# Down products m4, m5 and m7: the half-filled last chunk laid on both partition halves, two matmuls for it instead of three

## The reference, cut to what matters

```
mod = silu(c) @ wmod                        # six vectors per batch
x = x + ga * ((layernorm(x)*(1+ca)+sa) @ masked_weight.T)
h = layernorm(x)*(1+cb)+sb
u = silu(h @ w1.T) * (h @ w2.T)             # 2048 x 2752; w1, w2, w3 are 4-bit codes with scales
x = x + gb * (u @ w3.T)                     # the down product: 2752 summed over, 1024 out
```

## Time and profile before

| what | us |
|---|---|
| median of three runs | 1569.66 |
| span of the profiled execution | 1567.6 |
| down stage, first to last matmul | 1144.7 to 1563.7 |
| TensorE busy in the span | 1539.4 |
| VectorE busy in the span | 1029.5 |

### The profile page before, as it was taken

The page is one execution under the profiler, slowest core; times in us unless marked ns, Lnnn a source line. Parts: engine busy times, 40 slices in busy tenths (PEclk is TensorE's granted clock), DMA queues, the critical chain, the costliest instruction groups (busy, mean ns, idle before and its releaser), DMA issues.

```text
span 1567.6 us, 19154 instructions
## 1 busy us (share of the span) xinstructions
PE 1539.4 (98%) x7200; PEld 1269.6 (81%) x7200; DVE 1029.5 (66%) x1486; ACT 989.6 (63%) x1290; POOL 5.5 (0%) x10
## 2 busy tenths in 40 slices
PE   5899999999999999999999999999999999999999
PEld 3688888888888888888888888888888888888887
DVE  5687786555555455547676666666875757956994
ACT  3475676998888888884898988785433432333220
POOL 0000000000000000000000000000000000000000
PEclk9999999999999999999999999999999999999999
DMA  9976423564555445532778787786777868947973
GB/s 368 372 258 228 134 81 138 177 200 166 186 169 187 153 162 180 178 128 97 257 228 252 207 250 208 207 254 171 260 292 272 332 204 302 343 160 268 397 279 122
DMA packets 170139, 345.97 MB, mean 221 GB/s; under 512 B 14752, under 2 KB 65344, under 8 KB 170048
## 3 DMA queue, kind: packets, MB, share of 16 engines
q1 hardware_dynamic: 170048, 344.76, 65.1%
HBM read 249.77 MB, written 94.93 MB: 220 GB/s over the span
## 4 chain that ended last, share of the span: by engine, by line
PE 96%; DMA 2%; DVE 0%; ACT 0%; SPq 0%; issue 0%
PE ps L1916 10%; PE ps L1915 10%; PE ps L1914 10%; PE ps L1988 9%; PE ps L1987 9%; PE ps L1989 9%; PE ps L1925 9%; PE ps L1927 9%; PE ps L1926 9%; PE ps L1832 4%; PE ps L1834 4%; PE ps L1833 4%; DMA wmod<-wmod 2%; PE ps L1789 2%; PE ps L1772 1%; DVE attn_w_lo L1368 0%
## 5 line engine op out<-in xcount | busy, mean ns | idle before, releaser
L861 ACT ACTIVATE w_raw<-w_raw 128x1024 f32<-128x1024 f32 x287 | 304.6, 1061 | 9.1
L1914 PE MATMUL ps<-ffn_in_hi,w_hi 128*128 128x512 f32 x688 | 268.6, 390 | 0.0
L1916 PE MATMUL ps<-ffn_in_hi,w_lo 128*128 128x512 f32 x688 | 267.8, 389 | 0.0
L1915 PE MATMUL ps<-ffn_in_lo,w_hi 128*128 128x512 f32 x688 | 267.7, 389 | 0.0
L1987 PE MATMUL ps<-t_hi,s_hi 128*128 128x512 f32 x616 | 239.6, 389 | 0.0
L1988 PE MATMUL ps<-t_lo,s_hi 128*128 128x512 f32 x616 | 239.6, 389 | 0.0
L1989 PE MATMUL ps<-t_hi,s_lo 128*128 128x512 f32 x616 | 239.6, 389 | 0.0
L1925 PE MATMUL ps<-x_m_hi,stream_hi 128*128 128x512 f32 x604 | 235.0, 389 | 0.0
L1926 PE MATMUL ps<-x_m_lo,stream_hi 128*128 128x512 f32 x604 | 235.0, 389 | 0.0
L1927 PE MATMUL ps<-x_m_hi,stream_lo 128*128 128x512 f32 x604 | 235.0, 389 | 0.0
L1114 ACT ACTIVATE s_hi<-s_raw 128x1408 fp32r<-128x1408 f32 x56 | 77.4, 1383 | 241.2 <-DVE s_raw L1624 192.6
(11 more groups left out here) (136 smaller groups left out, 2078.1 us busy)
## 6 DMA issues: line engine op xcount, KB each, us to landing
s_raw<-h_d SPq DMA_DIRECT2D x96, 704.0 KB, 5.6
stream_raw<-t_d SPq DMA_DIRECT2D x150, 256.0 KB, 3.4
t_d<-combined SPq DMA_DIRECT2D x106, 256.0 KB, 2.6
wmod<-wmod SPq DMA_DIRECT2D x12, 2048.0 KB, 15.3
t_raw<-w_d SPq DMA_DIRECT2D x88, 256.0 KB, 6.1
w_codes<-w12q SPq DMA_DIRECT2D x41, 512.0 KB, 5.3
h_d<-h_tile SPq DMA_DIRECT2D x44, 256.0 KB, 2.4
h_d<-up_c SPq DMA_DIRECT2D x44, 256.0 KB, 3.3
```

The source lines that it names most:

```text
L861: act.activation(RAWF[r], RAWF[r] if j else RQ[r][:], ACT.Prelu, bias=bias, scale=sign, alpha=slope).then_inc(line_ready, 1)
L1914: pe.matmul(acc, RH[r][:, k, :], HH[:, b, k, :], start=(k == 0), stop=False)
L1915: pe.matmul(acc, RH[r][:, k, :], HL[:, b, k, :], start=False, stop=False)
L1916: last = pe.matmul(acc, RL[r][:, k, :], HH[:, b, k, :], start=False, stop=(k == C - 1))
```

## The change

A list `SHORT_K` marks m4, m5 and m7. For these:
- `load_s` takes 10 chunks in one DMA, and the last chunk's 64 filled rows in a second one whose source is read twice, `[2, 64, 128]`, so that they land on partitions 0 to 63 and again on 64 to 127.
- `load_t` reads the last chunk's 64 filled rows twice, `[2, 64, columns]`, in the same way.
- `s_low` writes S_lo of the last chunk over the lower half of S_hi, and S_lo of the other ten as before: two instructions.
- `t_low` sets the lower half of T_lo's last chunk to zero and subtracts the upper 64 rows.
- `down_tile` then needs two matmuls for the last chunk: (S_hi over S_lo) x (T_hi twice) and (S_hi over S_lo) x (T_lo over zero).

```diff
...
     TWO_S = [len(p[1]) == 2 for p in PRODUCTS]
     TWO_T = [len(p[3]) == 2 for p in PRODUCTS]
     COPIES = 4
+    SHORT_K = [p[0] in ("m4", "m5", "m7") for p in PRODUCTS]
 
     def s_adds(m):
         return sum(JT for i in range(m // JT) if TWO_S[i]) + (m % JT + 1 if TWO_S[m // JT] else 0)
 
     def s_loads(m):
-        return 16 * sum(len(PRODUCTS[n // JT][1]) for n in range(m % 4, m + 1, 4))
+        return 16 * sum(len(PRODUCTS[n // JT][1]) * (2 if SHORT_K[n // JT] else 1) for n in range(m % 4, m + 1, 4))
 
     def one_row(i):
         blocks = PRODUCTS[i][3]
...
                 sp.wait_ge(w3_combined, j + 1)
                 sp.dma_start(w3_d[j * P:(j + 1) * P, :], E3[j % 3][:]).then_inc(w3_stored[j % 3], 16)
 
+            def twice(rows):
+                return rows.unsqueeze(0).broadcast_to([2, TAIL, rows.shape[1]])
+
             def load_s(m):
                 p = m % 4
                 if m >= 4:
...
                 blocks = PRODUCTS[m // JT][1]
                 for n, (r, half) in enumerate(blocks):
                     tile = (half - 1) * TILES + (r - 1) * JT + m % JT
-                    sp.dma_start(SR[p][:, 1 - n].rearrange("p c k -> p (c k)"),
-                                 h_d[tile * P:(tile + 1) * P, :]).then_inc(s_raw_loaded[p], 16)
+                    if SHORT_K[m // JT]:
+                        sp.dma_start(SR[p][:, 1 - n, 0:HC - 1].rearrange("p c k -> p (c k)"),
+                                     h_d[tile * P:(tile + 1) * P, 0:(HC - 1) * P]).then_inc(s_raw_loaded[p], 16)
+                        sp.dma_start(SR[p][:, 1 - n, HC - 1],
+                                     twice(h_d[tile * P:tile * P + TAIL, (HC - 1) * P:HC * P])).then_inc(s_raw_loaded[p], 16)
+                    else:
+                        sp.dma_start(SR[p][:, 1 - n].rearrange("p c k -> p (c k)"),
+                                     h_d[tile * P:(tile + 1) * P, :]).then_inc(s_raw_loaded[p], 16)
+
+            def w3_rows_of(i, k, row, cols):
+                if SHORT_K[i] and k == HC - 1:
+                    return twice(w3_d[row:row + TAIL, cols])
+                return w3_d[row:row + P, cols]
 
             def load_t(i, u):
                 if i >= 2:
...
                 for k in UNITS[u]:
                     if one_row(i):
                         row = ((blocks[0][0] - 1) * HC + k) * P
-                        sp.dma_start(TR[place(i)][k][:].rearrange("p a n -> p (a n)"), w3_d[row:row + P, :]).then_inc(t_raw_loaded[u], 16)
+                        sp.dma_start(TR[place(i)][k][:].rearrange("p a n -> p (a n)"), w3_rows_of(i, k, row, slice(0, D))).then_inc(t_raw_loaded[u], 16)
                     else:
                         for n, (half, d) in enumerate(blocks):
                             row = ((half - 1) * HC + k) * P
-                            sp.dma_start(TR[place(i)][k][:, 1 - n, :], w3_d[row:row + P, (d - 1) * HALF:d * HALF]).then_inc(t_raw_loaded[u], 16)
+                            sp.dma_start(TR[place(i)][k][:, 1 - n, :], w3_rows_of(i, k, row, slice((d - 1) * HALF, d * HALF))).then_inc(t_raw_loaded[u], 16)
 
             def finish_w3(j):
                 store_w3(j)
...
             def s_low(m):
                 p = m % 4
                 dve.wait_ge(s_hi, m + 1)
-                dve.tensor_tensor(SL[p][:], SR[p][:, 1], SH[p][:].bitcast(F32), ALU.subtract).then_inc(s_lo, 1)
+                if SHORT_K[m // JT]:
+                    dve.tensor_tensor(SH[p][TAIL:P, HC - 1, :], SR[p][TAIL:P, 1, HC - 1], SH[p][TAIL:P, HC - 1, :].bitcast(F32), ALU.subtract)
+                    dve.tensor_tensor(SL[p][:, 0:HC - 1], SR[p][:, 1, 0:HC - 1], SH[p][:, 0:HC - 1].bitcast(F32), ALU.subtract).then_inc(s_lo, 1)
+                else:
+                    dve.tensor_tensor(SL[p][:], SR[p][:, 1], SH[p][:].bitcast(F32), ALU.subtract).then_inc(s_lo, 1)
 
             def t_add(i, k):
                 if TWO_T[i]:
...
 
             def t_low(i, k):
                 dve.wait_ge(t_hi, i * HC + k + 1)
-                dve.tensor_tensor(TL[place(i)][k][:], TR[place(i)][k][:, 1, :], TH[place(i)][k][:].bitcast(F32), ALU.subtract).then_inc(t_lo, 1)
+                rows = P
+                if SHORT_K[i] and k == HC - 1:
+                    rows = TAIL
+                    dve.memset(TL[place(i)][k][TAIL:P, :].bitcast(F32), 0.0)
+                dve.tensor_tensor(TL[place(i)][k][0:rows, :], TR[place(i)][k][0:rows, 1, :], TH[place(i)][k][0:rows, :].bitcast(F32),
+                                  ALU.subtract).then_inc(t_lo, 1)
 
             def t_units(i, units):
                 for k in units:
...
                     if j == 0:
                         pe.wait_ge(t_lo, i * HC + k + 1)
                     pe.matmul(acc, SH[p][:, k, :], TH[place(i)][k][:], start=(k == 0), stop=False)
-                    pe.matmul(acc, SH[p][:, k, :], TL[place(i)][k][:], start=False, stop=False)
-                    last = pe.matmul(acc, SL[p][:, k, :], TH[place(i)][k][:], start=False, stop=(k == HC - 1))
+                    short = SHORT_K[i] and k == HC - 1
+                    last = pe.matmul(acc, SH[p][:, k, :], TL[place(i)][k][:], start=False, stop=short)
+                    if not short:
+                        last = pe.matmul(acc, SL[p][:, k, :], TH[place(i)][k][:], start=False, stop=(k == HC - 1))
                 last.then_inc(m_done, 1)
 
             for m in range(MTILES):
```

## The result

The changed kernel takes 1594.05 us, the kernel before 1569.66 us in the same comparison: ratio 1.0154, interval 1.0141 to 1.0166, so 24.4 us slower. Forecast were 1597.5 us. The profiled execution has a span of 1591.6 us, 24.0 more than before.

The account below looks back on a forecast made before the run. TensorE's chain of waits (96%) was taken as the bound. Two engines with 158 us of tail work from 1419.8 would end tile 55 at 1591.5, the span at 1595.4: 1569.66 + 27.8 = 1597.5 us, range 1564 to 1616.

Parts of the forecast that it names:

- Two engines per tail: Tail loads with source [2, 64, n] run on two of 16 DMA engines, 64 rows each instead of eight.
- What the two engines have to carry, 158 us from tile 37 on: From tile 37 to 52 the two engines have 158 us of work, where TensorE's 16 tiles take 116.
- The place of the waits: TensorE waits for s_low from about tile 41: tiles 10 to 11 us apart in m5, about 8 in m7.
- The size: The whole kernel's span grows by 27.8 us over 1567.6, giving 1597.5 us; forecast chance 0.60.
- m4 gives its 1.8 us with 3 us of cover left: In m4, tile 16's s_low ends about 1261.5, TensorE wants it at 1264.4; eight tiles save 1.8 us.
- SyncE, "Nothing": On SyncE's queue, 40 more DMAs for S add 0.4 to 0.8 us a tile of issues, costing nothing.
- VectorE adds 0.07 us a tile: Splitting s_low into 128 and 1280 elements adds 0.07 us on VectorE in each of 24 tiles.
- rival 1: All 16 engines take the new DMAs; only VectorE in m5 is late: 4.4 us gained, 1565.2 us; chance 0.18.
- rival 3: Two engines, and TensorE's clock falls while waiting in m5: 3.9 us more per such tile, four give 1613; chance 0.11.
- A DMA share under 0.8 in m5: Sign of being right: the DMA share, 0.96 before, falls below 0.8 in m5's stage.

Follow-up runs that it names:

- e3: The change with only S tails on the twice-read source; T tails loaded by two DMAs of 64 rows each: 1582.85 us, ratio 1.0079 to the kernel before.
- e4: The change with only the four T tails on the twice-read source; S tails loaded by two DMAs of 64 rows each: 1576.83 us, ratio 1.0042.
- e1: The change with every 64-row tail loaded by two DMAs of 64 rows, one per partition half: 1568.12 us, ratio 0.9985 to the kernel before.
- e9: e1 with each tail source viewed as [2, 32, n] with every other row, which can't be folded: 1595.06 us, ratio 1.0154 to the kernel before.
- e7: e1 without VectorE's additions (no split s_low, no memset), leaving out S's low part in the last chunk: 1566.83 us, ratio 0.9982.
- e11: e1 with hi and lo stacked on T's side, so s_low is one instruction again: 1566.98 us, ratio 0.9977 to the kernel before.
- e10: e1 with each tail source viewed as [4, 16, n] with rows interleaved, which can't be folded: 1576.82 us, ratio 1.0037 to the kernel before.
- e5: e1 with each tail source viewed as [2, 32, n], the same 64 rows in order: 1568.56 us, interval 0.9981 to 0.9999.

## Why the prediction was right

- **Two engines per tail** (the step on which all hung): right. Packets of the change (+24), of e3 (+144) and e4 (+1224), the return of the time in e1, and its full loss in e9 show it. The rule that it was read from, the outermost dimension's count, held for 2 and 4 as well.
- **What the two engines have to carry, 158 us from tile 37 on**: near. The first of these loads was issued at 1420.18, and S of tile 55 was there at about 1574.3 (VectorE's add), 154 us later; forecast were 159 with the first packet's delay, for which no row stood. m7's round, forecast 8.1 us, was 7.5 to 7.8, m5's, forecast 10.6, was 10.3 to 10.8 in tiles 42 to 44. The likeliest cause is that 0.029 us a row was a little high; no run prices it alone.
- **The place of the waits**: mostly right. 10 to 11.6 us from tile to tile in m5 from tile 43, and a wait of 9.6 at tile 48, 7 us more than the 2.6 of each tile before it, where some 8 more were forecast. The first pauses, 0.3 us each, stand at tiles 41 and 42. Wrong was "about 8 in m7": tiles 48 to 55 ran without a listed wait. At tile 48 TensorE had stood so long that three tiles of S were on their way; the excess of 0.5 us a tile ate that lead, and tile 55 began only 0.3 to 0.4 us behind its s_low. The end is the same, the path differs.
- **The size**: 24.4 us measured, 27.8 forecast. S of tile 55 came at 1574.3 instead of 1578.8, 4.5 us less; from there tile 55 took 6.0 us to start instead of 5.4. That is the whole difference of the profiled spans, 24.0 against 27.8.
- **m4 gives its 1.8 us with 3 us of cover left**: the cover was wrong. s_low of tile 16 ended at 1264.5, not 1261.5, and TensorE waited 0.45 us. VectorE could take up the T tail at 1260.0, not at about 1257; the two T tails' issues alone took SyncE 4.6 us. Why they landed 3 us late is not shown.
- **SyncE, "Nothing"**: failed as put. Issues behind the tails took up to 4.2 us, and one 9.2. In e1, with more DMAs on 16 engines, that is gone, so the count of DMAs isn't the cause. It is taken as the same cause seen from another queue; no run holds SyncE back without the two engines, or the reverse, so its own share is open.
- **VectorE adds 0.07 us a tile**: failed, 0.29 us against e1's rows. It hardly mattered in the change, which waits for transfers. In e1 it is the reason read from the rows for 1568.1 instead of rival 1's 1565.2; e7 and e11, without the split, got back about 1 us of it in the medians, within the overlap of the intervals.
- **The clock** (rival 3) came in part: 19 matmuls at the lower level, 3.9 us, behind waits of 3.5 and 9.6 us; behind waits of 2.6 it stayed up. The length of the wait alone doesn't decide: in e10 it fell behind one of 1.9. The 3.9 us are a term of the balance, but hardly one on top of the forecast: tile 55 began at most 0.4 us behind its s_low, so what a full clock had saved would, by the forecast's own argument, have turned into waits for S.
- **A DMA share under 0.8 in m5**: failed, 0.85 (what the 14 other engines did, the profile doesn't tell apart). The GB/s, 290 against 369, told more.

The rows say where the 0.29 us lie. Larger instructions start 0.08 to 0.09 us before the one ahead of them has ended (1.62 us with a step of 1.53, 0.69 with 0.60). Beside the 64 x 128 subtraction that overlap is missing twice: 0.68 us with a step of 0.71, then 0.29 with 0.30. The forecast took its 0.07 us from steps that have the overlap in them. What stays open is why it is missing here.

## What to carry to other kernels

Look at the outermost dimension of both sides of each DMA before counting its bytes: the same tails cost this kernel 26 us on two engines and nothing that could be seen on 16, and a loop of two DMAs of 64 rows mends it. The profile shows the number of engines without naming one: small packets per DMA. Where work has to be added to a tight engine, the operand that is made once per product is the better place than that made once per tile: three T chunks against 24 tiles of S. e11 against e1 points that way, by 1.1 us that the intervals don't separate.

## What the runs showed of the hardware that was not expected

- DMAs that run on few engines hold up their issuer as well: SyncE's issues behind the tails took up to 4.2 us in m5, and one 9.2, with 1.25 at most before and none of it in e1.
- A view with an outermost 2 that can be folded into its neighbour keeps 16 engines (e5: 16096 small packets); one that can't gets two (e9: 14864), with the same rows and bytes.
- The instruction of 64 x 128 takes a step of 0.30 us, where 128 elements at 1.04 ns and the 0.07 us found from the larger ones give 0.20, and the step ahead of it is 0.71 instead of 0.60.
- GpSimd's sum of 128x512 takes 1.29 us at best, and slows VectorE by 1.10 us in one of its 0.69 us instructions.
